# Grouped attention: transposed probabilities and values as rounded high and low parts, and the causal masks issued behind the four score products

## The reference, cut to what matters

```
q  = x @ w_q                 # 16 heads of 128, scaled by 128 ** -0.5
k, v = split(x @ w_kv)       # 4 heads of 128 each
scores = q @ k.T             # for each batch and head, 512 x 512
scores = where(causal, scores, -inf)
probs  = softmax(scores)
ctx    = probs @ v
out    = ctx @ w_dense       # then x = layernorm(x + out)
```

## Time and profile before

| what | value |
|---|---|
| median of three runs | 1938.15 us |
| the profiled execution's own time | 1940.06 us |
| its span, first to last instruction | 1938.1 us |
| mean granted TensorE clock | 0.898 of full speed |
| PE busy | 1609.6 us, 83% of the span |
| DVE busy | 1067.0 us, 55% |
| ACT busy | 882.2 us, 46% |
| POOL busy | 359.4 us, 19% |

### The profile page before, as it was taken

How to read it: one execution, slowest core, us unless ns; L and a number is a source line. 1 busy time by engine, 2 the same in 40 slices (tenths; PEclk the granted TensorE clock), 3 DMA queues, 4 the chain that set the end, 5 groups by cost and what they waited for, 6 DMA issues and landing times. The chain is left out here.

```text
span 1938.1 us, 27116 instructions
## 1 busy us (share of the span) xinstructions
PE 1609.6 (83%) x9439; PEld 1283.2 (66%) x9441; DVE 1067.0 (55%) x2018; ACT 882.2 (46%) x1895; POOL 359.4 (19%) x305
## 2 busy tenths in 40 slices
PE   7489959999987899975766639759999999985866
PEld 6478846676767688873544426747878878774855
DVE  3555435446445444444566651347777777776354
ACT  3333325455444333332544422336666666657433
POOL 0035521101013245534111010211011001000400
PEclk9689979999999799987788766989999999998968
DMA  1241110000000823202443010000000000001010
GB/s 53 51 136 51 37 60 17 17 0 16 0 0 0 208 74 97 79 4 56 53 44 40 12 51 1 1 28 17 11 15 16 16 8 16 8 1 44 0 45 22
DMA packets 74939, 68.11 MB, mean 35 GB/s; under 512 B 31024, under 2 KB 66056, under 8 KB 74864
## 3 DMA queue, kind: packets, MB, share of 16 engines
q1 hardware_dynamic: 72208, 64.57, 12.8%
q0 software_dynamic: 2400, 2.30, 1.4%
q10 hardware_dynamic: 256, 0.26, 0.0%
HBM read 56.46 MB, written 1.21 MB: 30 GB/s over the span
## 5 line engine op out<-in xcount | busy, mean ns | idle before, releaser
L2125 ACT ACTIVATE diff_att_probs<-psum,diff_att_neg_max 128x512 f32<-128x512 f32 x256 | 175.2, 701 | 25.6 <-DVE diff_att_neg_max L2186 25.6
L2186 DVE TENSOR_REDUCE diff_att_neg_max<-psum 128x2 f32<-128x1024 f32 x128 | 155.6, 1217 | 38.5 <-PE psum L2023 38.4
L99 PE MATMUL psum<-fin_w_hi,fin_h_hi 128*128 128x256 f32 x352 | 108.4, 308 | 47.8 <-POOL fin_w_lo L266 47.8
L2044 PE MATMUL psum<-diff_att_v_tok,diff_att_mixed_t 128*128 128x128 f32 x1024 | 130.3, 282 | 2.7 <-ACT diff_att_mixed_t L2131 2.7
L2044 PEld LDWEIGHTS psum<-diff_att_v_tok,diff_att_mixed_t 128*128 128x128 f32 x1024 | 121.9, 195 | 14.3 <-issue 14.3
L99 PEld LDWEIGHTS psum<-fin_w_hi,fin_h_hi 128*128 128x128 f32 x352 | 74.1, 211 | 52.4 <-DVE fin_h_lo L278 50.1
L100 PE MATMUL psum<-fin_w_lo,fin_h_hi 128*128 128x256 f32 x352 | 105.8, 301 | 0.0
L101 PE MATMUL psum<-fin_w_hi,fin_h_lo 128*128 128x256 f32 x352 | 105.3, 299 | 0.0
L1576 PE MATMUL psum<-mla_att_k_feat,mla_att_q_own 128*128 128x128 f32 (+3 forms) x128 | 47.8, 454 | 66.3 <-ACT mla_att_probs L1683 61.5
L1683 ACT ACTIVATE mla_att_probs<-psum,mla_att_neg_max 128x128 f32<-128x128 f32 (+3 forms) x128 | 65.7, 528 | 73.8 <-DVE mla_att_neg_max L1735 72.5
L1206 DVE TENSOR_REDUCE gqa_neg_max<-psum 128x1 f32<-128x128 f32 (+3 forms) x128 | 56.1, 483 | 72.8 <-PE psum L1124 72.8
(11 more groups left out here) (435 smaller groups left out, 4549.6 us busy)
## 6 DMA issues: line engine op xcount, KB each, us to landing
top_wb<-top_w_dram SPq DMA_DIRECT2D x16, 384.0 KB, 4.3
golden_wb<-golden_w_dram SPq DMA_DIRECT2D x8, 512.0 KB, 4.6
top_wb<-top_w_dram SPq DMA_DIRECT2D x16, 256.0 KB, 4.0
mla_att_k_feat<-mla_att_parts SPq DMA_DIRECT2D x56, 64.0 KB
top_w_nat<-in_L_ffn_w SPq DMA_DIRECT2D x16, 192.0 KB, 2.9
top_w_nat<-in_L_ffn_v SPq DMA_DIRECT2D x16, 192.0 KB, 4.3
top_down_w<-in_L_ffn_w SPq DMA_DIRECT2D x1, 3072.0 KB, 13.1
golden_down_w<-in_L_ffn_Wd SPq DMA_DIRECT2D x1, 2048.0 KB, 8.8
```

Of the source, the lines that this page charges most:

```text
L99: nc.tensor.matmul(out, s_hi, m_hi, start=start, stop=False)
L2044: last = nc.tensor.matmul(bank[6][:, qt * P:(qt + 1) * P], mixed_t[:, u % 2, kt, qt * P:(qt + 1) * P], v_tok[:, slot, b * QT + kt, :], sta ...
L2125: last = nc.scalar.activation(probs[:, qt, m, :], bank[2 * (qt % 2) + m], ACT.Exp, bias=neg_max[:, qt, m:m + 1], accum_out=row_sum[:, qt, ...
L2186: nc.vector.tensor_reduce(neg_max[:, qt, :], psum[:, 2 * (qt % 2):2 * (qt % 2) + 2, :], AX.X, ALU.max, negate=True).then_inc(maxed, 1)
```

## The change

It does four things, all in `grouped_attention`:

- The transposed probabilities of key tiles 0, 1 and 2 are kept as `pt_hi` and `pt_lo` (fp32r), the values as `v_hi` and `v_lo`, and `attend` makes three fp32r products for each of these tiles. Key tile 3, 128 wide, stays one float32 product of `v_last` and `pt_last`.
- ACT writes the high parts of key tiles 0 and 1. DVE writes that of tile 2 and the copy of tile 3, and then makes three low parts by subtraction from PSUM, in the order tile 2, tile 0, tile 1.
- The four mask products of a unit stand behind its four score products.
- ACT's read of a value projection becomes two (the last 128 columns to `v_last`, all to `v_hi`), and DVE makes `v_lo` by a subtraction (`split_v`). The projection that takes the bank next waits for it. POOL's tile of zeros shrinks to one number a partition, read as a broadcast.

```
-        zeros = st.sb("zeros", [P, DC, HPG * HD])
+        zeros = st.sb("zeros", [P, 1, 1])
-        v_tok = st.sb("v_tok", [P, NT, HD])
+        v_last = st.sb("v_last", [P, BATCH, HD])
+        v_hi, v_lo = (st.sb(f"v_{n}", [P, NT, HD], F32R) for n in ("hi", "lo"))
-        probs_t = st.sb("probs_t", [P, QT, SEQ])
+        pt_hi, pt_lo = (st.sb(f"pt_{n}", [P, QT - 1, SEQ], F32R) for n in ("hi", "lo"))
+        pt_last = st.sb("pt_last", [P, P])
...
-                        nc.gpsimd.tensor_tensor(hi[:], raw[:], zeros[:, :, 0:raw.shape[2]], ALU.add).then_inc(w_rounded, 1)
+                        nc.gpsimd.tensor_tensor(hi[:], raw[:], zeros[:].to_broadcast([P, DC, raw.shape[2]]), ALU.add).then_inc(w_rounded, 1)
...
                         pe.wait_ge(proj_read, g * JOBS + (j - 2))
+                        if jobs[j - 3][0] == "v":
+                            pe.wait_ge(v_split, g * 2 + (jobs[j - 3][2] + 1))
...
                         nc.tensor.matmul(bank[qt][:, 0:(qt + 1) * P], q_feat[...], k_feat[...], start=True, stop=False)
+                    for qt in range(QT):
                         nc.tensor.matmul(bank[qt][:, qt * P:(qt + 1) * P], env.identb[:], env.causal[:],
                                          start=False, stop=True).then_inc(scores_made, 1)
...
-                    pe.wait_ge(t_read_act, g * UNITS + (u + 1))
                     pe.wait_ge(t_read_dve, g * (2 * UNITS) + 2 * (u + 1))
+                    pe.wait_ge(v_split, g * 2 + 2)
...
-                    for kt in range(QT):
-                        last = nc.tensor.matmul(bank[6][:, kt * P:SEQ], v_tok[:, b * QT + kt, :],
-                                                probs_t[:, kt, 0:SEQ - kt * P], start=kt == 0, stop=kt == QT - 1)
+                    for kt in range(QT - 1):
+                        cols = slice(0, SEQ - kt * P)
+                        product3(nc, bank[6][:, kt * P:SEQ], (v_hi[:, b * QT + kt, :], v_lo[:, b * QT + kt, :]),
+                                 (pt_hi[:, kt, cols], pt_lo[:, kt, cols]), start=kt == 0, stop=False)
+                    last = nc.tensor.matmul(bank[6][:, (QT - 1) * P:SEQ], v_last[:, b, :], pt_last[:], start=False, stop=True)
...
-                        read = nc.scalar.activation(v_tok[...], job_bank(j), ACT.Copy)
-                    read.then_inc(proj_read, 1)
+                        nc.scalar.activation(v_last[:, half, :], job_bank(j)[:, (QT - 1) * P:], ACT.Copy).then_inc(proj_read, 1)
+                        read = nc.scalar.activation(v_hi[...], job_bank(j), ACT.Copy)
+                    read.then_inc(v_high if kind == "v" else proj_read, 1)
...
-                        nc.scalar.activation(probs_t[:, 0, :], bank[4][:], ACT.Copy).then_inc(t_read_act, 1)
+                        nc.scalar.activation(pt_hi[:, 0, :], bank[4][:], ACT.Copy).then_inc(t_high_act, 1)
+                        act.wait_ge(t_made, g * (3 * UNITS) + (3 * u + 2))
+                        nc.scalar.activation(pt_hi[:, 1, 0:3 * P], bank[5][:, 0:3 * P], ACT.Copy).then_inc(t_high_act, 1)
...
+                def split_v(g, half):
+                    tiles = slice(4 * half, 4 * half + 4)
+                    dve.wait_ge(v_high, g * 2 + (half + 1))
+                    nc.vector.tensor_tensor(v_lo[:, tiles, :]..., job_bank(V_JOBS[half]),
+                                            v_hi[:, tiles, :]..., ALU.subtract).then_inc(v_split, 1)
...
                 with dve.Fori(0, GROUPS) as g:
+                    split_v(g, 0)
                     maxima(g, 0)
+                    split_v(g, 1)
                     normalise(g, 0)
                     for u in range(UNITS):
                         if u + 1 < UNITS:
                             maxima(g, u + 1)
-                        dve.wait_ge(t_made, g * (3 * UNITS) + (3 * u + 2))
-                        nc.vector.tensor_copy(probs_t[:, 1, 0:3 * P], bank[5][:, 0:3 * P]).then_inc(t_read_dve, 1)
                         dve.wait_ge(t_made, g * (3 * UNITS) + (3 * u + 3))
-                        nc.vector.tensor_copy(probs_t[:, 2, 0:2 * P], bank[7][:, 0:2 * P])
-                        nc.vector.tensor_copy(probs_t[:, 3, 0:P], bank[7][:, 2 * P:3 * P]).then_inc(t_read_dve, 1)
+                        nc.vector.tensor_copy(pt_hi[:, 2, 0:2 * P], bank[7][:, 0:2 * P]).then_inc(t_high_dve, 1)
+                        nc.vector.tensor_copy(pt_last[:], bank[7][:, 2 * P:3 * P])
+                        dve.wait_ge(t_high_dve, g * UNITS + (u + 1))
+                        nc.vector.tensor_tensor(pt_lo[:, 2, 0:2 * P], bank[7][:, 0:2 * P], pt_hi[:, 2, 0:2 * P]..., ALU.subtract).then_inc(t_read_dve, 1)
+                        for kt, width in ((0, SEQ), (1, 3 * P)):
+                            dve.wait_ge(t_high_act, g * (2 * UNITS) + (2 * u + kt + 1))
+                            last = nc.vector.tensor_tensor(pt_lo[:, kt, 0:width], bank[4 + kt][:, 0:width], pt_hi[:, kt, 0:width]..., ALU.subtract)
+                        last.then_inc(t_read_dve, 1)
                         if u + 1 < UNITS:
                             normalise(g, u + 1)
```

More of the change, by code:

```diff
@@ L1053, in grouped_attention @@
             inverted, probs_ready = sem("inverted"), sem("probs_ready")
[L1054 removed]
+            t_made, t_high_act, t_high_dve, t_read_dve = sem("t_made"), sem("t_high_act"), sem("t_high_dve"), sem("t_read_dve")
+            v_high, v_split = sem("v_high"), sem("v_split")
             ctx_made, ctx_read = sem("ctx_made"), sem("ctx_read")
@@ L1060, in grouped_attention @@
             jobs += [("q", h, half) for h in range(1, HPG) for half in range(2)]
+            V_JOBS = [j for j, job in enumerate(jobs) if job[0] == "v"]
             EARLY = 4
@@ L1167, in read_projection @@
                     else:
-                        read = nc.scalar.activation(v_tok[:, 4 * half:4 * half + 4, :].rearrange("p t e -> p (t e)"), job_bank(j), ACT.Copy)
-                    read.then_inc(proj_read, 1)
+                        nc.scalar.activation(v_last[:, half, :], job_bank(j)[:, (QT - 1) * P:], ACT.Copy).then_inc(proj_read, 1)
+                        read = nc.scalar.activation(v_hi[:, 4 * half:4 * half + 4, :].rearrange("p t e -> p (t e)"), job_bank(j), ACT.Copy)
+                    read.then_inc(v_high if kind == "v" else proj_read, 1)
                 def exps(g, u, *qts):
@@ L1217, in normalise @@
                     last.then_inc(probs_ready, 1)
+                def split_v(g, half):
+                    tiles = slice(4 * half, 4 * half + 4)
+                    dve.wait_ge(v_high, g * 2 + (half + 1))
+                    nc.vector.tensor_tensor(v_lo[:, tiles, :].rearrange("p t e -> p (t e)"), job_bank(V_JOBS[half]),
+                                            v_hi[:, tiles, :].bitcast(F32).rearrange("p t e -> p (t e)"), ALU.subtract).then_inc(v_split, 1)
                 with dve.Fori(0, GROUPS) as g:
+                    split_v(g, 0)
                     maxima(g, 0)
+                    split_v(g, 1)
                     normalise(g, 0)
@@ L1224, in _ @@
                             maxima(g, u + 1)
-                        dve.wait_ge(t_made, g * (3 * UNITS) + (3 * u + 2))
-                        nc.vector.tensor_copy(probs_t[:, 1, 0:3 * P], bank[5][:, 0:3 * P]).then_inc(t_read_dve, 1)
                         dve.wait_ge(t_made, g * (3 * UNITS) + (3 * u + 3))
-                        nc.vector.tensor_copy(probs_t[:, 2, 0:2 * P], bank[7][:, 0:2 * P])
-                        nc.vector.tensor_copy(probs_t[:, 3, 0:P], bank[7][:, 2 * P:3 * P]).then_inc(t_read_dve, 1)
+                        nc.vector.tensor_copy(pt_hi[:, 2, 0:2 * P], bank[7][:, 0:2 * P]).then_inc(t_high_dve, 1)
+                        nc.vector.tensor_copy(pt_last[:], bank[7][:, 2 * P:3 * P])
+                        dve.wait_ge(t_high_dve, g * UNITS + (u + 1))
+                        nc.vector.tensor_tensor(pt_lo[:, 2, 0:2 * P], bank[7][:, 0:2 * P], pt_hi[:, 2, 0:2 * P].bitcast(F32),
+                                                ALU.subtract).then_inc(t_read_dve, 1)
+                        for kt, width in ((0, SEQ), (1, 3 * P)):
+                            dve.wait_ge(t_high_act, g * (2 * UNITS) + (2 * u + kt + 1))
+                            last = nc.vector.tensor_tensor(pt_lo[:, kt, 0:width], bank[4 + kt][:, 0:width], pt_hi[:, kt, 0:width].bitcast(F32),
+                                                           ALU.subtract)
+                        last.then_inc(t_read_dve, 1)
                         if u + 1 < UNITS:
```

## The result

The changed kernel's median is 1945.3 us over 20 runs, that of before 1937.31 over its 20 runs; the ratio is 1.0041 with a 95% interval of 1.0026 to 1.0055. That is 8.0 us slower (5 to 11). Forecast were 8.0 us, from 1938.15 to 1946.1. The profiled execution's span is 1944.3 us, mean clock 0.897.

A forecast was written before the change was run, and what follows sets the result against it. PE was taken to bound the kernel before, DVE and ACT the changed turn. Groups 2.0, POOL 4.7 and clock 1.3 make +8.0 on the profiled 1940.06, 1948.1; the median lies 1.91 lower, 1946.1 us, range 1934 to 1956.

The forecast's parts named there:

- The turn: From one attend to the next: 5.50 us instead of 5.85, set by DVE and ACT, not by PE's 5.35.
- PE's work: PE's products in one turn: attend 2.21 to 1.84, scores with masks 2.55 to 2.42, in all 5.85 to 5.35 us.
- The tail: Each group's end: last attend 3.39 us after the last transposes start, where 2.11 stood; some 1.3 lost twice.
- The first turn: Each group's first turn: the first maximum waits for all four masks, at 2.65 us instead of some 0.6, losing 0.35.
- the groups: Turns, first turn and tail of each group together: net 0.5 us later, 2.0 for four groups.
- POOL: Unit 1's multiplications wait for POOL's end in groups 0 to 2: 9.0 us against 4.3, so 4.7 more.
- The rival's point: In rival (a), chance 0.13: unit 1's multiplications may come after POOL has ended, so today's waits of 4.3 us go.
- The new subtractions: DVE's low parts, one input in PSUM, stay free of POOL's lock; if locked, up to 2.4 us a group, 7 in all.
- Clock: Longer PE idle times in tails and beside POOL bring the lower clock: 1.3 us more than today, ends 0 and 12.
- Rival (c): Each tail and POOL wait brings the low clock back, seven times 1.7 us: 10 more, 1956; chance 0.17.
- The edits at nothing: `split_v` and the smaller memset, priced at no cost; uncovered, `split_v`'s subtractions would cost about 0.7 us each, 5.6 in all.

The follow-up runs named there:

- parts_only: The changed kernel with each mask again directly behind its score product; 1943.9 us, ratio 1.0045 to the kernel before.
- one_first: late_fill with ACT's high copy of key tile 0 ahead of the next unit's last exp, that of tile 1 behind it; 1926.1 us, ratio 0.9949.
- late_fill: The changed kernel with both the later POOL split of late_split and the unused products of fill_idle; 1928.4 us, ratio 0.995.
- late_split: The changed kernel with POOL splitting the next group's weights only after a group's last multiplications; 1937.4 us, ratio 1.0005.
- masks_only: The kernel before with only the four masks of a unit moved behind its four score products; 1930.0 us, ratio 0.997.
- masks_late: The kernel before, float32 attend kept, with grouped masks, one-number zeros and POOL's split after a group's last multiplications; 1927.3 us, ratio 0.9939.
- fill_idle: The changed kernel with 32 unused bf16 products behind each of a group's last two sets of transposes; 1940.8 us, ratio 1.0011.

## Why the prediction was right

**The turn.** Forecast 5.50, set by DVE and ACT; measured 5.47. From the start of the maxima at 530.16 the high copy of tile 0 ends at 2.98 (3.02 in the sum), attend starts at 4.22 (4.25), the next maxima at 5.48 (5.50). parts_only (0.03 more for 0.16 of PE's work) and one_first (0.13 less from the order on ACT alone, down to PE's own 5.34, where 5.35 was forecast) show that the pace was not PE's. The margin was small, 0.13. In steady turns half of DVE's wait is put down to the transposes, 0.26 at 532.10; both lie in the time before ACT's copy ends.

**PE's work.** Attend was to be 1.84 and is 1.88 to 1.91, since the first fp32r product behind float32 or bf16 takes 0.31 to 0.34 instead of 0.24 to its next. A 384-wide one takes 0.17. Masks 0.23 as said.

**The tail.** 3.39 forecast from the last transposes to the last attend, 3.36 measured; 3.66 for the unit before, 3.56 measured. The first turn: 6.2 forecast, 6.17 measured in group 3. Without POOL and clock (late_fill) a group's unit part is 44.9 against 44.2, and attend is 0.3 shorter: some 0.3 later in each group, not 0.5. The scores of unit 0, which the sum left out, also get 0.15 shorter in each group. So the groups cost 0.5 in all instead of 2.0.

**POOL.** The multiplications were to end 4.1, 2.5 and 2.4 later and end 3.3, 2.6 and 2.5 later (4.59, 3.87, 3.77 less 1.27): 8.4 instead of 9.0. late_split showed that all of it was on the path. For before the sum took PE's idle times, 4.3; from attend to attend the two waits lengthen a turn by 2.37 each (8.22 against 5.85; the 9.88 of group 2 holds 1.7 of the clock too), so 4.7. The net is 3.7, not 4.7. The rival's point, that POOL might be missed altogether, did not come. The new subtractions were not held by POOL: the two at 305.27 in group 0 take 1.16 beside POOL's pass from 305.59 to 307.49, as in a turn without POOL.

**Clock.** This is the term that was mis-sized, and by far: it was put at 1.3 more than before's 1.7, and it is 6.1 more, the largest of the three. Against late_fill, which has no fall of the clock in this stage and no POOL wait, the changed stage is 16.1 longer; 8.4 of it are the multiplications, the other 7.7 the clock's. They are found behind the POOL wait of group 0 (0.8), on the three ways to the next group (1.5 each), in group 3's last turn (6.89 against 5.28, so 1.6) and in its last attend (0.7). The direction was in the text. Rival (c) was near: it had seven falls, one at each tail and each POOL wait, and there were six, two of them in group 3's tail; the two shorter POOL waits, 1.91 and 1.82, were spared here. (Its 1956 should have been 1955, since its 10 take the place of the 1.3.)

**What I had left out.** Adding a broadcast number makes POOL's high pass of 1024 elements 1.90 instead of 2.34, so its whole split is 0.56 shorter, once at the stage's start on PE's path. Together: 0.5 for the groups, 3.7 for POOL and 6.1 for the clock make the stage's 10.3; less the 0.56 ahead of it the whole should be near 9.7, within the measured 5 to 11. The path and the waits were as forecast, but that the sum fell on the median to 0.1 is luck: a clock term too small by 4.8 stood beside others too large by 2.5, and falls of the clock differ from one execution to the next.

**The edits at nothing.** `split_v` was covered: the way from a group's first scores to those of unit 1 is 14.95, it was 15.1. masks_only, without `split_v`, has 14.95 too, and parts_only, with it, 15.1.

## What to carry to other kernels

When an engine without slack is relieved by giving work to one with slack, write out the loop through the second engine, with each wait at its place in the in-order queues, before counting the saving. The places that have no overlap, first and last turn of each group, pay the longer chain in full. Slack also hides shocks: POOL's blocking of DVE cost nothing in group 0 as long as DVE had 1.8 us to spare, and all of it afterwards. A change that joins a gain and a loss should be split and each half measured: the masks alone were worth some 6 us (2 to 10), and together with the other half nothing that could be told. And where a change makes idle times longer, price the clock at each of them: here it was the largest term.

## What the runs showed of the hardware that I had not expected

- Idle times of PE of 2.30 and 2.11 us with 3 us of work between were followed by the lower clock level in all four tails of the changed kernel (9.43 us to the next scores against 7.9) and in three of four in late_split. With 2.10 twice, in parts_only, it was one of four. Idle times of 0.85 in the tails of before, masks_only and masks_late were never followed by it. Filling 1.8 us of each with products kept the clock at 1.00 in all 16 tails of the four kernels that did so.
- The length of an idle time did not settle it. Beside POOL the clock fell behind 2.64 in the changed kernel and behind 1.91 in fill_idle, but not behind 1.91 in the changed kernel, nor behind 2.27 and 2.28 in masks_only. Which of them is hit stays open.
- POOL's tensor_tensor ran faster when its second input was one number a partition read as a broadcast: 1.90 against 2.34 us for 1024 elements, 0.61 against 0.72 for 256.
- A product that had to wait for a later exp turned a steady pace into an alternating one (5.38, 5.67) with nearly the same mean as before the edit; the mean alone would have looked like no effect.
